# Attention and recurrent layer on one core: key sums in two row halves and two banks from slot 36 on

## The reference

```python
x = x + xattn(layernorm(x), ctx, ctx, W_proj, b_proj)
x = x + ffn(layernorm(x), wf, uf, bf, wi, ui, bi, wc, uc, bc, wo, uo, bo, in_c)
# xattn: 16 heads of 32, keys at a distance of at most 64 rows,
#   y = softmax(q k^T / sqrt(32)) v ; y @ W_proj.T + b_proj
# ffn: for each of the 8 batches in turn (512 rows at once)
#   c = sigmoid(x wf.T + c uf.T + bf) * c + sigmoid(x wi.T + c ui.T + bi) * tanh(x wc.T + c uc.T + bc)
# then tanh(x wo.T + c_final uo.T + bo)
```

## Time and profile before

| what | value |
|---|---|
| median of three runs | 942.4 us |
| span of the profiled execution (the page gives no other time of it) | 941.8 us |
| PE, DVE, ACT, POOL busy | 98%, 72%, 51%, 22% |
| chain that ended last | PE 85%, DVE 6%, issue 3%, ACT 2%, DMA 2% |
| exps, ACT line 901, x512 | 239.4 us |
| masks, DVE line 1013, x512 | 166.1 us |
| side blocks, DVE line 1048, into keys, x420 | 125.6 us |
| value, PE line 774, x864, and line 779 on keys, x736 | 43.4 and 32.4 us |
| multiply, DVE line 1058, x23 | 15.8 us |

### The profile page before, as it was taken

The page is one execution under the profiler, slowest core; times in us unless marked ns, Lnnn a source line. Parts: engine busy times, 40 slices in busy tenths (PEclk is TensorE's granted clock), DMA queues, the critical chain, the costliest instruction groups (busy, mean ns, idle before and its releaser), DMA issues.

```text
span 941.8 us, 21981 instructions
## 1 busy us (share of the span) xinstructions
PE 918.6 (98%) x7842; PEld 715.5 (76%) x7842; DVE 676.1 (72%) x2281; ACT 476.5 (51%) x1430; POOL 204.8 (22%) x228
## 2 busy tenths in 40 slices
PE   7999999899999999999999999999999999999998
PEld 5555567678877788887887888788877888878887
DVE  6888898788779977998799878987798531143222
ACT  6888666655455544645565555555655321131222
POOL 5475322211101111111111111111101100003444
PEclk9999999999999999999999999999999999999999
DMA  9464232234444453544443444433333150059862
GB/s 305 161 192 150 88 96 69 87 89 126 135 111 134 119 143 96 135 110 124 130 141 112 121 114 122 115 107 110 97 98 91 50 163 0 1 179 382 307 237 101
DMA packets 139348, 123.58 MB, mean 131 GB/s; under 512 B 46824, under 2 KB 104168, under 8 KB 137704
## 3 DMA queue, kind: packets, MB, share of 16 engines
q1 hardware_dynamic: 138520, 121.91, 42.6%
q10 hardware_dynamic: 720, 0.27, 0.2%
HBM read 87.70 MB, written 34.46 MB: 130 GB/s over the span
## 4 chain that ended last, share of the span: by engine, by line
PE 85%; DVE 6%; issue 3%; ACT 2%; DMA 2%; POOL 1%; SPq 0%; DVEq 0%; ACTq 0%; POOLq 0%
PE ps_g L684 18%; PE ps_g L686 17%; PE ps_g L685 17%; PE ps_a L731 5%; PE ps_a L753 4%; PE ps_m L684 3%; PE ps_v L774 3%; PE ps_m L686 3%; PE ps_m L685 3%; PE ps_m L806 2%; PE ps_a L684 2%; PE ps_v L779 2%; DVE probs L1013 2%; PE ps_a L686 2%; PE ps_a L685 2%
## 5 line engine op out<-in xcount | busy, mean ns | idle before, releaser
L901 ACT ACTIVATE probs<-probs,rowmin 128x192 f32<-128x192 f32 (+1 forms) x512 | 239.4, 470 | 114.3 <-DVE rowmin L1013 114.3
L1013 DVE CUSTOM_DVE_ANT_0 probs<-ps_a,mask 128x192 f32<-128x192 f32 (+1 forms) x512 | 166.1, 386 | 31.7 <-PE ps_a L731 30.6
L684 PE MATMUL ps_g<-state_hi,gate_w 128*128 128x512 f32 x336 | 133.6, 398 | 0.0
L686 PE MATMUL ps_g<-state_hi,gate_w 128*128 128x512 f32 x336 | 131.1, 390 | 0.0
L685 PE MATMUL ps_g<-state_lo,gate_w 128*128 128x512 f32 x336 | 130.9, 389 | 0.0
L1048 DVE STREAM_TRANSPOSE keys<-probs 32x128 f32<-32x128 f32 x420 | 125.6, 299 | 5.2
L948 ACT ACTIVATE gate<-ps_g,bias 128x512 f32<-128x512 f32 x84 | 57.6, 686 | 105.7 <-PE ps_g L686 105.2
L901 ACT ACTIVATION_READ_ACCUMULATOR probs<-probs,rowmin 128x1 f32 x512 | 96.3, 188 | 0.0
L663 POOL TENSOR_TENSOR attn_lo<-recip,attn_hi 128x512 fp32r<-128x512 f32 x23 | 29.8, 1294 | 276.8 <-ACT attn_hi L914 276.8
L906 ACT ACTIVATE probs_t<-ps_a 128x512 f32<-128x512 f32 x108 | 59.3, 595 | 52.3 <-PE ps_a L753 52.3
L684 PE MATMUL ps_g<-x2t_even,gate_w 128*128 128x512 f32 x192 | 80.0, 417 | 0.0
(11 more groups left out here) (211 smaller groups left out, 1722.4 us busy)
## 6 DMA issues: line engine op xcount, KB each, us to landing
values<-ctx_rows SPq DMA_DIRECT2D x34, 256.0 KB, 4.3
xr<-x SPq DMA_DIRECT2D x32, 256.0 KB, 3.8
keys<-ctx_t SPq DMA_DIRECT2D x16, 512.0 KB, 4.2
x_dram<-xr SPq DMA_DIRECT2D x32, 256.0 KB, 2.6
gate_w<-x2t_dram SPq DMA_DIRECT2D x8, 1024.0 KB, 9.8
keys<-ctx_t SPq DMA_DIRECT2D x16, 384.0 KB, 3.4
x2t_dram<-x2t_even SPq DMA_DIRECT2D x12, 512.0 KB, 4.1
x2t_dram<-x2t_odd SPq DMA_DIRECT2D x12, 512.0 KB, 4.4
```

What stands on the lines that cost most here:

```text
L684: pe.matmul(ps, lhs[0], rhs[0], start=start, stop=False)
L686: return pe.matmul(ps, lhs[1], rhs[0], start=False, stop=stop)
L901: act.activation(row, row, ACT.Exp, bias=rowmin[:, i % 2, h:h + 1], scale=-1.0, accum_out=rowsum[:, i // G % 2, i % G, h:h + 1]).then_inc( ...
L1013: dve.tensor_tensor_reduce(probs[:, i % 2, h, 0:SEEN[t]], ps_a[h][:, score_at[i]:score_at[i] + SEEN[t]], mask[:, MASK0[t]:MASK0[t] + SEEN[ ...
```

## The change

From slot 36 on, the sum over keys is cut into two row halves of 64 keys. The lower 64 rows of the array sum into ps_v, the upper 64 into ps_m, in tiles of 64x32; each side product covers only the 64 queries that see those keys, and is left out where there is no neighbour. ACT copies ps_m to SBUF, DVE adds ps_v, then multiplies by the reciprocals. What used ps_m moves into score banks: the projection and turned x2 into ps_a3, one turned query tile into ps_a2. Waits on `masked`, `x1_done` and `x2_lo` guard those banks. In the step list, the turns of x2 stand right behind the probability turns, the projection stands behind 4 unit products that follow the values, and residual and statistics stand behind both reciprocals, the send and the first side blocks.

```diff
             steps.extend(("turn", m) for m in both)
+            if s == 2 and i - 1 not in MOVED:
+                tile_steps("turn2", i - 1)
             ...
             cells(2)
             ...
             if s == 2 and i - 1 not in MOVED:
-                tile_steps("turn2", i - 1)
+                tile_steps("turn2_lo", i - 1)
             gates(2)
-            steps.extend(("score", m) for m in ahead[:1])
-            if s == 2 and i - 1 not in MOVED:
-                tile_steps("turn2_lo", i - 1)
-            steps.extend(("score", m) for m in ahead[1:])
+            steps.extend(("score", m) for m in ahead)
             ...
             steps.extend(("exp", m) for m in ahead)
             steps.extend(("value", m) for m in both)
+            if s == 2:
+                tile_steps("mult", i)
+            gates()
+            renew()
+            cells(4 if s == 0 else 3)
             if s == 0:
                 tile_steps("proj", i - 1)
             else:
-                tile_steps("mult", i)
-            gates()
-            renew()
-            cells(3)
-            steps.extend(("recip", m) for m in ahead[:1])
+                tile_steps("halves", i)
+            steps.extend(("recip", m) for m in ahead)
+            if s == 0:
+                tile_steps("send", i)
+            steps.extend(("sides", m) for m in ahead[:1])
             if s == 0:
                 tile_steps("resid", i - 1)
                 tile_steps("stat2", i - 1)
-            else:
-                tile_steps("halves", i)
-            steps.extend(("recip", m) for m in ahead[1:])
-            if s == 0:
-                tile_steps("send", i)
-            steps.extend(("sides", m) for m in ahead[:1])
...
-            cells(7)
+            cells(6 if s == 0 else 7)
...
+        value_ps = [ps_v, ps_m]
+        half_row = probs_t[:, 0:HPG, :].rearrange("p a q -> p (a q)")
+        proj_ps = [ps_m if i < SENT - 1 else ps_a[3] for i in range(TILES)]
+        x2_ps = [ps_m if i < SENT else ps_a[3] for i in range(TILES)]
+        query_ps = [ps_m if i <= SENT else ps_a[2] for i in range(TURNED_X)]
...
                 if kind == "score":
...
                         pe.wait_ge(turned_a, i - i % 2)
+                        if g == 0:
+                            pe.wait_ge(x1_done, tile - 1)
+                            if tile - 2 not in MOVED:
+                                pe.wait_ge(x2_lo, tile - 1)
...
                 if kind == "value":
...
+                    if i >= FIRST_TWO:
+                        if i == FIRST_TWO:
+                            pe.wait_ge(recip_out, SENT)
+                        sided = [tile % TT > 0, tile % TT < TT - 1]
+                        for a in range(2):
+                            rows = slice(WINDOW * a, WINDOW * (a + 1))
+                            for h in range(HPG):
+                                d = slice(g * P + HEAD * h, g * P + HEAD * (h + 1))
+                                pe.matmul(value_ps[a][HEAD * h:HEAD * (h + 1), g * P:(g + 1) * P],
+                                          values[rows, tile % 2, 0, d], own_home[i][rows, h, :],
+                                          start=True, stop=not sided[a])
+                        for a in range(2):
+                            if not sided[a]:
+                                continue
+                            rows = slice(WINDOW * a, WINDOW * (a + 1))
+                            for h in range(HPG):
+                                d = slice(g * P + HEAD * h, g * P + HEAD * (h + 1))
+                                mm = pe.matmul(value_ps[a][HEAD * h:HEAD * (h + 1),
+                                                           g * P + rows.start:g * P + rows.stop],
+                                               values[rows, tile % 2, 1, d], side_home[i][rows, h, rows],
+                                               start=False, stop=True)
+                        mm.then_inc(valued, 1)
+                        continue
...
                 if kind == "proj":
-                    need(pe, x2_lo, split_by(i))
+                    if i >= SENT - 1:
+                        pe.wait_ge(masked, HPG * min(G * (i + 2), SLOTS))
+                    else:
+                        need(pe, x2_lo, split_by(i))
...
                 if kind == "turn":
                     act.wait_ge(turned, i + 1)
                     need(act, valued, i - i % 2 if i >= FIRST_TWO else i)
+                    if i >= FIRST_TWO + G and i % G == 0:
+                        act.wait_ge(attn_t, i // G)
...
+                if kind == "mult" and i >= SENT:
+                    act.wait_ge(valued, G * (i + 1))
+                    act.activation(half_row, ps_m[:, :], ACT.Copy).then_inc(half_out, 1)
...
                     else:
+                        dve.wait_ge(half_out, i - SENT + 1)
+                        dve.tensor_tensor(half_row, ps_v[:, :], half_row, ALU.add).then_inc(halves_sum, 1)
+                        dve.wait_ge(halves_sum, i - SENT + 1)
                         dve.wait_ge(recip_in, DMA * (i - SENT + 1))
-                        dve.tensor_tensor(recip_row, ps_v[:, :], recip_row, ALU.mult).then_inc(attn_t, 1)
+                        dve.tensor_tensor(recip_row, half_row, recip_row, ALU.mult).then_inc(attn_t, 1)
```

More of the change, by code:

```diff
@@ L442, in bass_xattn_ffn @@
         masked = sem("masked"); inverted = sem("inverted"); inv_turned = sem("inv_turned"); padded = sem("padded"); banks_zero = sem("banks_zero"); turned_b = sem("turned_b"); cleared = sem("cleared")
-        attn_t = sem("attn_t"); x1_done = sem("x1_done")
+        attn_t = sem("attn_t"); halves_sum = sem("halves_sum"); x1_done = sem("x1_done")
         stat2 = sem("stat2"); aggr2 = sem("aggr2"); var2 = sem("var2"); x2_done = sem("x2_done"); x2_lo = sem("x2_lo"); x2_blocks = sem("x2_blocks")
@@ L450, in bass_xattn_ffn @@
         q_ready = sem("q_ready"); expd = sem("expd"); turned_a = sem("turned_a"); recip_out = sem("recip_out")
-        attn_round = sem("attn_round"); wp_hi = sem("wp_hi")
+        attn_round = sem("attn_round"); half_out = sem("half_out"); wp_hi = sem("wp_hi")
         x2_hi = sem("x2_hi"); w_hi = sem("w_hi"); gated = sem("gated"); c_hi = sem("c_hi")
@@ L704, in _ @@
                     if i > SENT:
-                        pe.wait_ge(x1_done, i - 1)
+                        pe.wait_ge(masked, HPG * G * i)
                     else:
@@ L708, in _ @@
                     for g in range(G):
-                        mm = pe.transpose(ps_m[:, g * P:(g + 1) * P], xn[:, g * P:(g + 1) * P], ident[:, :])
+                        mm = pe.transpose(query_ps[i][:, g * P:(g + 1) * P], xn[:, g * P:(g + 1) * P], ident[:, :])
                     mm.then_inc(q_turned, 1)
@@ L812, in _ @@
                         for k in range(G):
-                            mm = product(ps_m[:, :], (attn_hi[:, k, :], attn_lo[:, k, :]),
+                            mm = product(proj_ps[i][:, :], (attn_hi[:, k, :], attn_lo[:, k, :]),
                                          (proj_w[:, 0, k, :], proj_w[:, 1, k, :]), k == 0, k == G - 1)
@@ L820, in _ @@
                     for k in range(G):
-                        mm = pe.transpose(ps_m[:, k * P:(k + 1) * P], x2[:, k * P:(k + 1) * P], ident[:, :])
+                        mm = pe.transpose(x2_ps[i][:, k * P:(k + 1) * P], x2[:, k * P:(k + 1) * P], ident[:, :])
                     mm.then_inc(x2_turned, 1)
@@ L889, in _ @@
                     need(act, scored, G * i)
-                    act.activation(queries[:, :, :], ps_m[:, :].rearrange("p (g q) -> p g q", g=G), ACT.Copy)\
+                    act.activation(queries[:, :, :], query_ps[i][:, :].rearrange("p (g q) -> p g q", g=G), ACT.Copy)\
                        .then_inc(q_ready, 1)
@@ L930, in _ @@
                         act.wait_ge(x2t_out[b % 2], DMA * TT * (b // 2))
-                    act.activation(x2t[b % 2][:, 0, :, t * P:(t + 1) * P], ps_m[:, :].rearrange("p (k q) -> p k q", k=G),
+                    act.activation(x2t[b % 2][:, 0, :, t * P:(t + 1) * P], x2_ps[i][:, :].rearrange("p (k q) -> p k q", k=G),
                                    ACT.Copy).then_inc(x2_hi, 1)
@@ L1062, in _ @@
                     dve.wait_ge(xr_ready, i + 1)
-                    dve.tensor_tensor(row, ps_m[:, :], row, ALU.add).then_inc(x1_done, 1)
+                    dve.tensor_tensor(row, proj_ps[i][:, :], row, ALU.add).then_inc(x1_done, 1)
                 if kind == "stat2":
@@ L1098, in _ @@
                         continue
-                    dve.tensor_tensor(x2t[b % 2][:, 1, :, cols], ps_m[:, :].rearrange("p (k q) -> p k q", k=G),
+                    dve.tensor_tensor(x2t[b % 2][:, 1, :, cols], x2_ps[i][:, :].rearrange("p (k q) -> p k q", k=G),
                                       x2t[b % 2][:, 0, :, cols].bitcast(F32), ALU.subtract).then_inc(x2_lo, 1)
```

## The result

The changed kernel takes **1006.35 us** (median of 4 runs, 1006.05 to 1006.62) against 942.68 (4 runs): 1.067 times the time before, 95% interval 1.065 to 1.068. That is 63.7 us more, where 48.5 were forecast. The sign came out and so did the chain of waits; the time lies just above the top of the range (1005), and 15 us of the loss were not in the sum. The gain on PE that the forecast counted isn't there.

What follows compares the result with a forecast made beforehand. PE was taken to set the pace, with DVE as full around middle tiles. Stalls of 36 + 6 + 7 = 49 us, less 0.5 of PE's gain, added to 942.4 gave 991 us; range 957 to 1005.

Steps and rivals of the forecast that it cites:

- What bounds the kernel; slower: Tiles 9 to 31: PE, 98% busy, sets the pace, DVE equally full around middle tiles; chance of slower 0.89.
- Rival 1: Side blocks at t = 0 and 1: only DVE's direct shift costs PE, 19 us, giving 961; chance 0.15.
- rival 3: All waits are met because DVE's late work is needed later; PE's 5.3 us gain counts, giving 937; chance 0.07.
- rival 4: Waits and gain cancel, leaving the time the same within 0.3% (2.8 us); chance 0.04.
- PE's gain, 0.11 us per middle slot: Value steps on PE: cheaper side products save 5.3 us over 48 slots; waits for DVE leave only 0.5.
- Rival 2: New tiles don't stream eight at a time: 20 to 29 us more PE work, about 1005; chance 0.1.
- The sum's chain makes DVE 2.1 us later: Every round 2: ACT's copy behind the exps, then DVE's add and multiply, start side blocks at 482.9, not 480.79.
- POOL's attn_lo and ACT's rounding move with it: Round 2: both get later with the multiply but are needed a round later, costing nothing; without that cover about 2.1 us.
- The projection's wait, 2.5 to 3.5 us at t = 1: Round 0 on PE: projection, reached at 490.7, waits for masks ending 493.18; 2.5 us stall before any DVE lateness.
- Round 0 later by 1.6 at t = 1 and 2: Middle tiles: reciprocals precede residual and statistics, so DVE waits 1.6 us for the exps; edge tiles lose about nothing.
- Turned rows of t = 3, 1.4 us six times: PE turns x2 two products earlier, before DVE has finished x2: a 1.4 us PE stall in each of six tiles.
- The sum: Some 9 us per batch, four batches 36, tiles 9 to 12 about 6, tiles 28 to 31 about 7; total 49.

Runs made afterwards that it cites:

- e5_kept_awake: Changed kernel with 20 unread identity transposes on PE ahead of the projection's wait for the masks at t = 1; 1000.3 us.
- e7: Changed kernel with the upper half's sum in ps_m left out: no ACT copy, no DVE add, multiply reads ps_v alone; 976.05 us.
- e1: Changed kernel with its new order, banks and waits, but values and multiply as in the kernel before (no ACT copy, no add); 977.85 us.
- e10_dve_work_only: Kernel before with one more DVE copy of ps_v ahead of round 2's multiply, no ACT copy; 943.57 us, ratio 1.0004.
- e3_sum_only: Kernel before with the sum's chain alone: ACT copies ps_v behind the exps, DVE takes a maximum in the add's place, then multiplies; 973.28 us.
- e2_copy_between: Changed kernel with ACT's copy of ps_m moved between the exps of the two slots instead of behind both; 982.6 us.
- e6_rounded_x2_later: Changed kernel with ACT's rounding of turned x2 at t = 2 and 3 moved behind the copies of the turned probabilities; 1011.21 us.
- e12_sum_behind_sides: Changed kernel with DVE's add and multiply, and the rounding, moved behind the first side blocks of round 2; 1026.69 us.
- e11_x2_turn_later: Changed kernel with PE's turn of x2 (t = 3) behind two unit products again, as before the change; 1004.54 us.
- e9_residual_first: Changed kernel with residual and its statistics back between the two reciprocals in round 0; 1045.91 us.

## Where the prediction was right, and the step that failed

- **The step that failed: a stall priced at its idle time, at full clock.** The chain of waits held: the four kinds on PE add up to 46.5 us that the kernel before does not have, beside 48.5 forecast. What the sum had at nothing is what follows a stall. It took the full clock of the earlier trace rows as given; in the changed kernel the half level follows four of the five stalls of 2.65 to 2.69 us at the projection, 1.6 us each, 7.0 in all by the mean clock. e5_kept_awake gets 6.05 of them back with one edit and takes 1000.3 us, inside the range. The second sequel is the break itself, some 0.26 us a stall (below).
- **What bounds the kernel; slower.** Right. Before, DVE has no pause in the stretch, so lateness adds up; the loss stands round by round where it was put. Rival 1 (only the direct shift, 961), rival 3 (faster) and rival 4 fell with it.
- **PE's gain, 0.11 us per middle slot, of which nearly nothing is left.** The number, 0.5 us, was near by luck. The gain isn't lost in waits for DVE, as the working has it; it is there in the first slot of a round only, and the second one gives most or all of it back (rows at 647.83 and 607.47). Rival 2 gave nearly the right total, 1005, by 20 to 29 us more of PE work; e7 has 0.6 more than e1 over forty rounds. The floor of some 25 ns from start to start, which the Trainium skill states ("TensorE: Matmul & The Clock Gate", "Wait — 56ns, not 53.3ns?"), isn't seen for tiles of 64 rows either: the 32 instructions of a slot's step in 0.36 us (647.83 to 648.19) are 11 ns apart.
- **The sum's chain makes DVE 2.1 us later.** Right within 0.4. The side blocks start 623.66 - 621.49 = 2.17 us behind the end of the exps, before 480.79 - 480.66 = 0.13: 2.04 later. The pause before the add is 2.32, not 1.2 to 1.8, since the exps now end 1.64 behind DVE's last mask step (621.49 against 622.17 - 2.32 = 619.85) where it was 480.66 - 479.43 = 1.23; counted from the masks, DVE is 2.45 later. e10_dve_work_only finds nothing for DVE's work, e3_sum_only 30.9 us for the chain with ACT's copy, and e2_copy_between gives 23.8 back by the copy's place.
- **"POOL's attn_lo and ACT's rounding move with it; they ... cost nothing."** This failed too, by a small sum. The rounding's result is needed late, but it stands at the head of ACT's queue and waits 1.55 us there, and the state and turned copies behind it are needed at once. Of the scores' 9.1 us of waits 2.0 are this (five of 0.38 to 0.41 in round 2 of t = 0; 0.52 each in e3_sum_only, without any change of order); it is 0.41 of the 0.58 of tile 20's round 2. The 6.8 of the long ones are DVE's lateness in another place, by e1_order_only and by e6_rounded_x2_later. e12_sum_behind_sides, where the same wait is 3.0 us and ACT's gates behind it keep DVE, is 20 us slower.
- **"The new wait of ACT's turn on the multiply ... is met by then."** No row shows that wait itself binding, but only since the rounding ahead of it waits for the same multiply.
- **The projection's wait, 2.5 to 3.5 us at t = 1.** Right: 2.69. That e1_order_only has 2.36 and e2_copy_between 2.69 again fits the working, by which the stall is there before any lateness of DVE. Only the half clock behind it was left out.
- **Round 0 later by 1.6 at t = 1 and 2.** The pause is 1.67. But the round at t = 2 lost 3.39 where 1.9 was reckoned: 1.37 of it is the scores' wait, a wait that no step of the working had, and behind it is DVE's lateness (above).
- **Turned rows of t = 3, 1.4 us six times.** 1.31 to 1.35 five times and 0.55 once (7.2 in all, the fourth wait on PE), and e11_x2_turn_later shows that the place of PE's turn makes no difference. The round still lost 2.24; some 0.4 of it stand at the values, whose second slot starts 0.71 us behind the first (712.62 and 713.33 on PE) where it was 0.36, as its side blocks end at 713.18. And a stall costs more than its bracket. At the projection, 633.00 is the last start before the stall and 636.08 the next: 3.08, where 0.23 separate two starts in a stream, so 2.85 lost by a bracket of 2.69; and the next start is another 0.33 behind, not 0.23. That is 0.26 beyond the bracket.
- **The sum.** 48.5 forecast, 63.7 measured. An estimate from the rows: 46.5 us of brackets, 42 breaks at 0.26, so 10.9, and 7.0 of clock make 64.4. It holds only roughly, since 0.26 was read at the projection alone and some waits have no bracket. How the rest divides stays open. The range was too short above because the sequels of a stall were in no bound.

## What to carry to other kernels

Before an operation that joins two in-order engines is added, ask of both where in its queue it will stand and what is already behind it: the same row of work was free on DVE alone, cost 31 us with a copy behind ACT's exps, and most of the loss came back when that copy was made one slot's exps earlier. Read a saving to the start of what comes next, not to the end of the step itself: the first slot's 0.10 us were gone at the second slot's end. When a sum of stalls is made, add for each the cost of the break and, for the long ones, that of the lowered clock behind it.

## What the runs showed of the hardware beyond what was expected

- In dense work the granted clock fell to its half level behind idle stretches of 2.65 to 2.69 us in the changed kernel, and of 2.11 us in e3_sum_only: there 128x512 products 0.43 us apart follow four of the five waits of 2.11 at the values, and the clock part is 7.8 us. It isn't certain to fall: of the changed kernel's five rounds at t = 1 with such a stall four show the half level, while the one from 517.02 has the same work and took 17.85 us at clock 1.00.

```profile
517.02:534.87 17.85, 14.24 (x152) 11.07 (x152) 15.64 (x52) 7.03 (x21) 1.87 (x2) 1.00 0.33 102
```

- A granted clock of 0.993 over the span is invisible in the page's tenths and worth 7 us; one of 0.975 (e9_residual_first) is worth 26.6. The mean clock of each run is the first thing to compare between kernels with stalls.
- Twenty transposes into an unused part of a bank, ahead of a wait, held the clock at its full level: rest 1000.3 against 999.3, so they cost at most about 1 us in all.
